# Two layers of state-space scan, router and experts on one core: the setup stage dissolved into the first scan stage

## The chip, the cores and the metric

The kernel runs on one core of a Trainium2 chip. The metric is the device time of one execution in microseconds (us). Engines are named as the profile names them: PE (matrix products), PEld (its weight loads), DVE (vector), ACT (activations), POOL (GpSimd), SP (issues the DMAs; SPq is its queue).

## What is computed

Two transformer-like layers over 4 batches of 1024 tokens with 128 channels. Each layer has an attention-like mixer and a routed feed-forward, each behind a norm that is modulated by the batch's condition vector `c`. Only the start of layer 0 matters here:

```python
# modulation, per layer l:  m = silu(c_l) @ wmod_l      (4 batches x 6 blocks of 128)
# blocks: 0 shift, 1 scale, 2 gate of the mixer;  3 shift, 4 scale, 5 gate of the feed-forward
h  = layernorm(x) * (1 + scale) + shift
xz = h @ Wi.T;  xp, z = split(xz)
xp = silu(causal_conv(xp, conv_w, 4 taps) + conv_b)
x_dbl = xp @ Wx.T;  dlt, B, C = split(x_dbl)            # rank 64, 16 states, 16 states
delta = softplus(dlt @ Wdt.T + bdt);  A = -exp(A_log)
state[n] = exp(delta * A[:, n]) * state[n] + delta * B[n] * xp          # over time, 16 states n
y = sum_n C[n] * state[n] + xp * Dp
out = (y * silu(z)) @ Wo.T;   x = x + gate * out
```

A gate has its sign kept and its size held at 0.25 or more.

## The kernel before

The whole work of layer 0's mixer is in `mamba`. Before it stands `setup` (lines 51 to 242), a block of its own that ends with all engines meeting. `setup` loads every weight and the whole of `x` (one DMA of 2 MB ahead of all others), makes the norm of all four batches (`norm.moments`, `root` with Sqrt, `normalize`, `turn`, `write`; the result is `hT`, channels on partitions), makes the modulation twice (as columns, L159, for `shift` and `scale`; as rows spread over 128 partitions by products with a broadcast stationary operand, L165, for `gate`, `shift_row`, `scale_row`), folds the convolution's taps into the weights (`wc0`, `wc1`, L209 and L210), the skip weight into the identity (`diagD0`) and prepares layer 1's parameters.

`mamba` then works batch by batch. Channels (2 halves of 128) are on partitions and time runs along the free axis in two column halves of 512 (`NCOL`). A batch has 32 **units** (`UNITS`): 16 states for each column half. One unit g is: POOL `make_bu` (L701, `u` times the spread row B), ACT `state_decay` (L605, two exps of 512 into one of 5 PSUM buffers `decay`), DVE `scan` (L786, two of 512), then the product with row C by DVE (`times_c`, L794, two) or, in each fourth unit, by POOL (L711), and PE `add_state` (L484, product with the identity into `y_ps`), which PE makes two units later. SP loads the rows B and C of each unit from DRAM into 4 and 5 buffers (L405, L414). `h` has 6 buffers: DVE's product of unit g waits for PE's `add_state` of unit g - 6.

All engines run their instructions in the order written. Beside the units of batch b stand, at fixed unit numbers s, the pieces of batch b and b + 1, all through one PSUM bank `piece`, so that each waits until ACT has read the one before: z (s = 4 to 7), x of the next batch (8 to 11, 4 taps each), ACT's Silu block with two table loads (13), low (15, 16), v (17 to 20), Exp and Ln of softplus (22 to 24), DVE's `make_delta` (24, 25), POOL's `make_u` (26, 27), the gate (17), the output product (22). Batch 0 has no batch before it: its x, low, v pieces, softplus of both column halves, `make_delta` and `make_u` (L693) are made ahead of unit 0 (lines 532 to 537, 628 to 639).

`route` (from L857) follows; its SP part loads the experts (L1056) and stores the last batch's rows (L1058), and it ends with a wait for the loads (L1064).

Of the kernel before, what the change touches and what calls it, by code (L numbers as in the profile page):

```python
# [5 lines left out]
ALU = mybir.AluOpType  # L6
# [33 lines left out]
LATE = (16, 48)  # L40
# [10 lines left out]
def setup(nc, a, m):  # L51

    with ExitStack() as ctx:
        sb = lambda name, shape, dt=F32: ctx.enter_context(nc.sbuf_tensor("su_" + name, shape, dt))
        sem = lambda name: m.kept.enter_context(nc.semaphore("su_" + name))
        ps = ctx.enter_context(nc.psum_tensor("ps_setup", [P, 8, COL], F32))
        cw0 = sb("cw0", [P, TAPS, D_IN])
        cw1 = sb("cw1", [P, TAPS, D_IN])
        wmod = sb("wmod", [P, 2, 6 * P])
        win0 = sb("win0", [P, D_IN])  # L60
        wout_raw = sb("wout_raw", [P, HALVES, P])
        cT = sb("cT", [P, 2, NBATCH])
        scT = sb("scT", [P, 2, NBATCH])
        sig = sb("sig", [P, 2, NBATCH])
        alog0 = sb("alog0", [P, HALVES, N0])
        alog1 = sb("alog1", [P, HEADS])
        dp0 = sb("dp0", [P, HALVES])
        rms = sb("rms", [P, HALVES])
        gsign = sb("gsign", [P, 2, 2, NBATCH, P])
        gate_raw = sb("gate_raw", [P, 2, 2, NBATCH, P])  # L70
        small, big, s_act, s_modT, s_modB, s_v = (
            sem(n) for n in ("small", "big", "s_act", "s_modT", "s_modB", "s_v"))
        s_bank_read = sem("s_bank_read")
        s_x = sem("s_x")
        GATE_BANK = ((0, 2), (4, 6))
        ROW_BANK = ((3, 5), (7, 1), (0, 2))
        lng = sb("lng", [P, P])
        lnb = sb("lnb", [P, P])
        s_early = sem("s_early")

        norm = make_norm(nc, ctx, m, 0, 0, [ps[:, 3, :], ps[:, 5, :]])
        block = ctx.enter_context(nc.Block())
        n_small, n_big, n_early = [0], [0], [0]

        @block.sync
        def _(sp):
            def load(dst, src, s=small, n=n_small):
                sp.dma_start(dst, src).then_inc(s, 16)
                n[0] += 1
            sp.dma_start(m.X[:], a["L0_attn_x"].rearrange("b (j p) d -> p (b j) d", p=P)).then_inc(s_x, 16)  # L90
            for l, name in ((0, "L0"), (1, "L1")):
                load(cT[:, l, :], a[name + "_cT"], s_early, n_early)
                load(wmod[:, l, :], a[name + "_wmod"], s_early, n_early)
            load(m.ident[:], a["ident"], s_early, n_early)
            load(m.tri[:], a["tri"])
            load(m.beforeb[:], a["beforeb"])
            load(m.onesb[:], a["onesb"])
            load(m.counth[:], a["counth"].partition_broadcast(P))
            load(m.count[:], a["count"].partition_broadcast(P))
            load(m.ids[:], a["ids"])  # L100
            load(cw0[:], a["L0_conv_row"].partition_broadcast(P))
            load(cw1[:], a["L1_conv_row"][:, 0:D_IN].partition_broadcast(P))
            load(win0[:], a["L0_WiT"][:, 0:D_IN])
            load(m.wz0[:], a["L0_WiT"][:, D_IN:2 * D_IN])
            load(m.tap1[:], a["tap1"])
            load(m.win1[:], a["L1_attn_W_in"][:, D_IN:D_IN + COL])
            load(m.wz1[:], a["L1_attn_W_in"][:, 0:D_IN])
            load(m.wdt1[:], a["L1_attn_W_in"][:, D_IN + COL:D_IN + COL + HEADS])
            load(m.wx[:], a["L0_WxT"].rearrange("(j p) n -> p j n", p=P))
            load(m.wdt0[:], a["L0_WdtT"])  # L110
# [2010 lines left out]
```

## Time and profile before

| | us |
|---|---|
| median of 3 runs | 1272.58 (1270.6 to 1275.98) |
| the profiled execution's own time | 1274.55 |
| its span in the profile | 1272.7 |
| `setup`, from the start to its end | 0 to 49 |
| batch 0 ahead of its units | 49 to 85.04 |
| layer 0's 128 units | 85.04 to 561 |
| route, experts, layer 1 | 561 to 1272.7 |

The chain of the page is read back from the last instruction and shows only the last 2% of the span, so the head of the kernel is read from the timeline, the windows and the waits instead.

### The profile page before, as it was taken

The page shows a single profiled execution, that of the slowest core. Times are in us where ns is not written, and L with a number is a line of the kernel's source. Part 1 is how long each engine was busy: PE and PEld are TensorE (multiplying, and loading weights), DVE is VectorE, ACT ScalarE, POOL GpSimd, SP SyncE. Part 2 cuts the span into 40 slices and gives each one's busy share as a digit, 9 for nine tenths or more (in the row PEclk, how much of TensorE's full clock was granted, in tenths as well). Part 3 has the DMA queues.
Part 4 walks back from the last instruction along what each step waited for, and adds up shares of the span by engine and source line. Part 5 has one row for each costly group of instructions (what it writes and reads, how often), then busy time and mean ns, then how long its engine had stood idle before and what let it go on. Part 6 is the DMA issues. An engine that isn't in the chain of part 4 may idle for free. (4 is left out here: it accounts for less than half of the span.)

```text
span 1272.7 us, 14828 instructions
## 1 busy us (share of the span) xinstructions
PE 897.0 (70%) x4200; PEld 569.9 (45%) x4200; DVE 919.8 (72%) x1848; ACT 590.5 (46%) x1298; POOL 767.3 (60%) x509
## 2 busy tenths in 40 slices
PE   3757877987898686762599915777786978338940
PEld 3413333433443232341599912345464756228940
DVE  6448799979988999969476744586795978464522
ACT  2264654576557646420144411546647585215620
POOL 0059679968997999830566558365534545236636
PEclk9878987997999898975699966889987968658975
DMA  6035344534643455421133411121101111142223
GB/s 173 1 104 173 120 133 149 165 115 130 179 154 125 139 164 171 138 97 44 32 86 87 81 50 44 48 57 34 44 10 42 43 50 34 34 167 59 66 58 99
DMA packets 85664, 117.72 MB, mean 92 GB/s; under 512 B 12688, under 2 KB 42576, under 8 KB 85456
## 3 DMA queue, kind: packets, MB, share of 16 engines
q1 hardware_dynamic: 78928, 103.13, 26.5%
q0 software_dynamic: 6656, 13.64, 4.9%
q8 instruction: 35, 0.57, 0.2%
q14 instruction: 45, 0.37, 0.1%
HBM read 102.52 MB, written 14.22 MB: 92 GB/s over the span
## 5 line engine op out<-in xcount | busy, mean ns | idle before, releaser
L484 PE MATMUL y_ps<-ma_h,ident 128*128 128x512 f32 x512 | 272.6, 668 | 75.4 <-POOL ma_h L711 43.6
L701 POOL TENSOR_TENSOR ma_bu<-ma_u,ma_row_b 128x1024 f32<-128x1024 f32 x128 | 298.6, 2357 | 16.8 <-DVE decay_ps L786 16.6
L605 ACT ACTIVATE decay_ps<-ma_delta,negA 128x512 f32<-128x512 f32 x256 | 173.0, 688 | 100.2 <-DVE ma_h L794 96.7
L1102 POOL DMA_INDIRECT s_rows<-xs,take x112 | 126.2, 1126 | 135.9 <-POOLq L867 78.1
L484 PEld LDWEIGHTS y_ps<-ma_h,ident 128*128 128x128 f32 x512 | 102.5, 212 | 228.1 <-issue 104.3
L786 DVE TENSOR_TENSOR_SCAN decay_ps<-decay_ps,ma_bu 128x512 f32<-128x512 f32 x96 | 115.7, 1220 | 32.1 <-ACT decay_ps L605 27.4
L1119 PE MATMUL s_up_ps<-s_xt,s_w 128*128 128x128 f32 x896 | 125.4, 286 | 7.8 <-issue 6.5
L794 DVE TENSOR_TENSOR ma_h<-decay_ps,ma_row_c 128x512 f32<-128x512 f32 x192 | 129.7, 676 | 0.0
L786 DVE TENSOR_TENSOR_SCAN decay_ps<-decay_ps,ma_carry,ma_bu 128x512 f32<-128x512 f32 x96 | 121.2, 1279 | 0.0
L1119 PEld LDWEIGHTS s_up_ps<-s_xt,s_w 128*128 128x128 f32 x896 | 115.8, 202 | 8.6 <-issue 6.8
L1128 PE MATMUL s_out_ps<-s_w,s_ht 128*128 128x128 f32 x608 | 89.6, 283 | 7.2 <-DVE s_outs L1195 7.0
L711 POOL TENSOR_TENSOR ma_h<-ma_h,ma_row_c 128x1024 f32<-128x1024 f32 x32 | 75.2, 2350 | 26.2 <-DVE ma_h L786 24.9
L1408 POOL DMA_INDIRECT mi_y<-ys,where x64 | 66.9, 1045 | 36.3 <-POOLq L1078 18.6
L1128 PEld LDWEIGHTS s_out_ps<-s_w,s_ht 128*128 128x128 f32 x608 | 78.9, 197 | 9.1 <-DVE s_ht L1185 7.3
L1146 ACT ACTIVATE s_xt<-s_xt_ps 128x128 f32<-128x128 f32 x112 | 31.8, 284 | 107.8 <-PE s_xt_ps L1111 99.1
L1438 POOL TENSOR_TENSOR mi_mm<-mi_dec,mi_gm 128x512 f32<-128x512 f32 x32 | 43.9, 1373 | 60.4 <-DVE mi_gm L1817 33.7
L1431 POOL TENSOR_TENSOR mi_cts<-mi_cdec,mi_xbc 128x512 f32<-128x512 f32 x28 | 39.2, 1400 | 65.7 <-ACT mi_cdec L1661 65.6
L1178 DVE COPY s_w<-w 128x768 f32 (+1 forms) x112 | 70.9, 638 | 5.5 <-issue 1.7
L693 POOL TENSOR_TENSOR ma_u<-ma_delta,ma_xp 128x1024 f32<-128x1024 f32 x8 | 19.7, 2458 | 86.4 <-DVE ma_delta L805 86.4
L1480 PE MATMUL mi_pre<-hT,wc 128*128 128x512 f32 x128 | 62.3, 635 | 3.9 <-ACT mi_raw L1615 1.8
L1185 DVE TENSOR_TENSOR s_ht<-s_up_ps,s_act_g 128x256 f32<-128x256 f32 x72 | 30.5, 424 | 45.1 <-ACT s_act_g L1153 24.2
L1158 ACT ACTIVATE s_ht<-s_up_ps,s_w 128x128 f32<-128x128 f32 x160 | 45.8, 370 | 27.6 <-PE s_up_ps L1119 22.4
(300 smaller groups left out, 1780.1 us busy)
## 6 DMA issues: line engine op xcount, KB each, us to landing
ma_row_b<-bc_rows SPq DMA_DIRECT2D x128, 256.0 KB, 3.6
ma_row_c<-bc_rows SPq DMA_DIRECT2D x128, 256.0 KB, 3.3
mi_cs<-cs_rows SPq DMA_DIRECT2D x32, 256.0 KB, 3.4
ys<-s_outs SPq DMA_DIRECT2D x28, 256.0 KB
w<-in_experts SPq DMA_DIRECT2D x1, 4112.0 KB, 13.4
w<-in_experts SPq DMA_DIRECT2D x1, 3072.0 KB, 10.7
xs<-rows SPq DMA_DIRECT2D x4, 512.0 KB, 3.7
out<-X SPq DMA_DIRECT2D x8, 256.0 KB
```

Of the source, the lines that this page charges most:

```text
L484: mm = pe.matmul(y_ps[:, j, :], m.ident[:], h[g % HS][:, j, :], start=False, stop=True, skip_group_check=True)
L605: act.activation(decay[s % DS][:], delta[b % 2][:, j, col(c)], ACT.Exp, scale=m.negA0[:, j, n:n + 1]).then_inc(decay_done, 1)
L701: pool.tensor_tensor(bu[g % BUS][:], u[b % 2][:, :, col(c)], both(row_b[g % BS]), ALU.mult).then_inc(bu_done, 1)
L711: pool.tensor_tensor(hs[:], hs[:], both(row_c[g % CS]), ALU.mult).then_inc(pool_product_done, 1)
L786: dve.tensor_tensor_scan(dst, d[:], bu[g % BUS][:, j, :], past, ALU.mult, ALU.add).then_inc(scan_done, 1)
L794: dve.tensor_tensor(h[g % HS][:, j, :], decay[s % DS][:], row_c[g % CS][:], ALU.mult).then_inc(product_done, 1)
L1102: pool.indirect_dma_start(rows[s % ROWS][:], None, m.xs[layer], bass.IndirectOffsetOnAxis(ap=m.take[:, s:s + 1], axis=0)).then_inc(fetched ...
L1119: mm = pe.matmul(up_ps[s % 2][:, f * P:(f + 1) * P], w[s % WS][:, f * P:(f + 1) * P], xt[s % 2][:], start=True, stop=True)
L1128: mm = pe.matmul(out_ps[s % 2][:, 0:P], ht[s % HS][:, f * P:(f + 1) * P], w[s % WS][:, UP + f * P:UP + (f + 1) * P], start=(f == 0), stop= ...
L1178: dve.tensor_copy(w[s % WS][:], m.w[layer][:, bass.ds(expert, 1), :].rearrange("p o f -> p (o f)")).then_inc(copied, 1)
L1408: pool.indirect_dma_start(fetched_rows[G % FETCH][k][:, t, :], None, m.ys[0], bass.IndirectOffsetOnAxis(ap=m.where[:, k, T:T + 1], axis=0) ...
L1480: mm = pe.matmul(bank[:], weights, m.hT[:, n, c * COL + k:c * COL + k + COL], start=(k == taps[0]), stop=(k == taps[-1]))
```

## The change

`setup` and the class `Norm` are removed; `mamba(nc, a, m)` does their work.

- The order of SP's loads is new: `cT`, the two halves of batch 0's `x`, `wmod` of layer 0 and `ident`; then eight loads that batch 0's pieces need (`taps_loaded`); then `x` of batches 1 to 3; then thirteen others (`rest_loaded`). Thirteen more are issued in batch 1's units (`later_loaded`). `cw0`, `cw1`, `wmod`, `win0`, `wout_raw` lie in `delta[1]` and `u[1]`, the normed `x` of batches 0 and 1 in `h[0]` and `h[5]`.
- Ahead of unit 0: the moments, root (Ln and Exp) and norm of batch 0; the four x pieces; low and v of the first column half alone; softplus, delta and `u` (now by DVE) of that half; moments and root of batches 1 to 3. Between the decays of unit 0 and unit 1, ACT reads batch 1's two turned pieces and two pieces of modulation rows.
- Beside batch 0's units: low, v, softplus, delta and `u` of the second column half (s = 1 to 8); the norm of batches 2 and 3 on ACT (s = 9 to 12 and 17 to 20, two tiles a unit) with their turns on PE (13, 14 and 24, 25); the gates' sign and size on 4 partitions (`modulate_rows`, s = 3 to 8, DVE); POOL's layer 1 preparation (s = 4 to 10); `wo` times the gate (`weigh_out`, s = 18 to 21, DVE).
- The modulation rows are made once, on 4 partitions, stored to DRAM (`mod_rows`, at SP's g = 11) and loaded back spread over 128 partitions: three loads of 256 KB at g = 13, eight in `route` between the experts' load and the store of the last rows.

```diff
-def setup(nc, a, m):
...
+    FIRST_LOW, FIRST_V, FIRST_SOFT, FIRST_SUM, FIRST_U = 1, 2, 5, 7, 8
+    FIRST_HAT = {2: 9, 3: 17}
+    FIRST_TURN = {2: 13, 3: 24}
+    ROWS, STORE_ROWS, LOAD_ROWS, WEIGH_OUT, FIRST_MOD, LAYER1 = 3, 11, 13, 18, 12, 4
...
+    early_keys = [("turn", 0, 0), ("x", 0, 0), ("x", 0, 1), ("turn", 0, 1), ("x", 0, 2), ("low", 0, 0), ("x", 0, 3),
+                  ("v", 0, 0), ("v", 0, 1), ("turn", 1, 0), ("turn", 1, 1), ("mod", 0, 0), ("mod", 0, 1)]
...
+                if g == STORE_ROWS:
+                    store_modulation()
+                if g == LOAD_ROWS:
+                    load_modulation()
...
+            act.wait_ge(mod_loaded, 48)
+            act.activation(scT[:], cT[:], ACT.Silu).then_inc(act_prep, 1)
             act.preload_act_table_set("natural_log_exp_and_others")
+            first_root(0, slice(0, BT))
+            act.wait_ge(prep, SCALED)
+            for key in early_keys[:7]:
+                read_piece(key)
+            act.preload_act_table_set("natural_log_exp_and_others")
+            act.activation(m.negA0[:], m.negA0[:], ACT.Exp).then_inc(act_prep, 1)
+            first_root(1, slice(BT, TILES))
+            for key in early_keys[7:9]:
+                read_piece(key)
+            soften(0, 0)
+            soften_log(0, 0)
             for j in range(HALVES):
                 state_decay(0, j)
+            for key in early_keys[9:]:
+                read_piece(key)
...
-            make_u(0, 0)
             for g in range(LEAD):
                 make_bu(g)
-            make_u(0, 1)
...
+            dve.wait_ge(first_x, 32)
+            first_moments(slice(0, BT))
+            dve.wait_ge(mod_done, 1)
...
+            for t in range(BT // 2):
+                normalize(0, t)
+            dve.wait_ge(taps_loaded, 16 * 8)
+            for k in range(TAPS):
+                then_prep(dve.tensor_tensor(m.wc0[:, k, :], win0, cw0[:, k, :], ALU.mult))
+            for t in range(BT // 2, BT):
+                normalize(0, t)
...
+            make_delta(0, 0)
+            dve.wait_ge(delta_done, 1)
+            dve.tensor_tensor(u[0][:, :, col(0)], delta[0][:, :, col(0)], xp(0, 0)[:], ALU.mult).then_inc(u_done, 1)
+            dve.wait_ge(act_prep, OTHER_ROOT)
+            for t in range(BT):
+                normalize(1, t)
...
+                for dst, block in ((m.gate[:, 0, 1], 5), (m.gate[:, 1, 1], 11), (m.lng_gate[:], 12), (m.lnb_gate[:], 13),
+                                   (m.shift_row[:, 1], 6), (m.scale_row[:, 1], 7), (m.shift_row[:, 2], 9),
+                                   (m.scale_row[:, 2], 10)):
+                    sp.dma_start(dst, m.mod_rows[:, block, :].partition_broadcast(P)).then_inc(m.late, 16)
```

## Rows read from the trace of the kernel before

**Rows 1.** Windows: busy time per engine (instructions), granted clock, DMA share, GB/s.

```profile
0.00:49.00 49.00, 23.16 (x136) 21.44 (x136) 34.16 (x139) 13.08 (x22) 0.19 (x4) 0.92 0.42 113
49.00:82.67 33.67, 25.59 (x52) 10.33 (x52) 3.79 (x6) 18.16 (x25) 3.25 (x2) 0.85 0.23 51
...
103.70:137.00 33.30, 33.26 (x72) 14.57 (x73) 24.50 (x28) 14.27 (x31) 30.41 (x15) 0.92 0.55 166
...
148.50:208.00 59.50, 47.15 (x97) 18.06 (x98) 57.85 (x66) 30.95 (x48) 49.24 (x22) 0.83 0.42 135
```

**Rows 2.** Timeline, setup: start, duration, engine, instruction, count, idle before.

```profile
11.10 6.28 DVE L192 BATCH_NORM_STATS2 stats<-X 128x6 f32<-128x128 f32 x32 [11.10 <-DMA X<-in_L_attn_x]
...
13.76 5.28 PE L159 MATMUL ps_setup<-su_scT,su_wmod 128*128 128x4 f32 x24 [13.76 <-ACT su_scT L137]
...
21.32 2.14 DVE L281 TENSOR_SCALAR n_xn<-X,n_mean,n_rstd 128x128 f32<-128x128 f32 x8
...
31.90 1.47 ACT L299 ACTIVATE hT<-ps_setup,shift,scale 128x512 f32<-128x512 f32 x2
...
32.84 5.58 PE L290 MATMUL ps_setup<-ident,n_xn 128*128 128x128 f32 x24 [6.92 <-ACT hT L299]
```

**Rows 3.** Windows of L165's matmuls alone (columns as in the first group, PE's engines).

```profile
18.90:22.00 3.10, 3.10 (x14) 3.10 (x15) 1.00 0.95 223
22.00:24.80 2.80, 2.80 (x20) 2.80 (x18) 1.00 0.11 6
```

**Rows 4.** Timeline, batch 0 ahead of its units: the pieces and the softplus.

```profile
49.23 9.73 PE L441 MATMUL y_ps<-hT,wc 128*128 128x512 f32 x16 [4.26 <-PEq L53]
...
58.80 7.03 PE L441 MATMUL decay_ps<-hT,wc 128*128 128x512 f32 x16
...
66.58 1.28 ACT L630 ACT_TABLE_LOAD   x1
...
70.94 0.68 ACT L588 ACTIVATE ma_u<-y_ps,bdt 128x512 f32<-128x512 f32 x1
...
74.93 2.05 ACT L568 ACTIVATE ma_u<-ma_u 128x1024 f32<-128x1024 f32 x2
```

**Rows 5.** Timeline, from delta to the first scan.

```profile
79.10 1.22 DVE L805 TENSOR_TENSOR ma_delta<-ma_delta,ma_u 128x1024 f32<-128x1024 f32 x1
...
82.67 6.94 POOL L701 TENSOR_TENSOR ma_bu<-ma_u,ma_row_b 128x1024 f32<-128x1024 f32 x3
85.04 2.35 DVE L786 TENSOR_TENSOR_SCAN decay_ps<-decay_ps,ma_bu 128x512 f32<-128x512 f32 x2 [4.72 <-POOL ma_bu L701]
...
89.56 2.35 POOL L693 TENSOR_TENSOR ma_u<-ma_delta,ma_xp 128x1024 f32<-128x1024 f32 x1
```

**Rows 6.** Waits from 103.7 to 158: who waited for whom, total, times, longest.

```profile
DVE decay_ps L786 <- ACT decay_ps L605: 13.2, 5, 4.4
ACT ma_xp L657 <- PE piece_ps L441: 12.0, 4, 3.3
```

**Rows 7.** Timeline of batch 0's units: PE after POOL's product, unit 12, Silu block, gate.

```profile
103.74 3.78 PE L484 MATMUL y_ps<-ma_h,ident 128*128 128x512 f32 x4 [8.59 <-POOL ma_h L711]
...
128.04 1.22 DVE L786 TENSOR_TENSOR_SCAN decay_ps<-decay_ps,ma_bu 128x512 f32<-128x512 f32 x1
...
134.84 7.03 PE L484 MATMUL y_ps<-ma_h,ident 128*128 128x512 f32 x16
...
138.16 1.28 ACT L677 ACT_TABLE_LOAD   x1
...
157.35 1.23 DVE L800 TENSOR_TENSOR ma_sz<-y_ps,ma_sz 128x1024 f32<-128x1024 f32 x1 [1.65 <-PE y_ps L484]
```

**Rows 8.** Timeline: a DVE sum with two SBUF inputs while POOL works.

```profile
186.63 2.15 DVE L805 TENSOR_TENSOR ma_delta<-ma_delta,ma_u 128x1024 f32<-128x1024 f32 x1
```

**Rows 9.** DMA issues (KB each, us to landing) and timeline rows of route.

```profile
ma_row_b<-bc_rows SPq DMA_DIRECT2D x128, 256.0 KB, 3.6
...
608.89 0.23 DVE L1051 TENSOR_SCALAR take<-r_take_ps 128x72 uint32<-128x72 f32 x1
```

More of the change, by code:

```diff
@@ new lines, in mamba @@
+    early_keys = [("turn", 0, 0), ("x", 0, 0), ("x", 0, 1), ("turn", 0, 1), ("x", 0, 2), ("low", 0, 0), ("x", 0, 3),
+                  ("v", 0, 0), ("v", 0, 1), ("turn", 1, 0), ("turn", 1, 1), ("mod", 0, 0), ("mod", 0, 1)]
+    place, placed = {}, {}
+    for key in early_keys:
+        place[key] = len(place)
+    for b in range(NBATCH):
+        for s in range(UNITS):
+            placed[b, s] = len(place)
+            for key in pieces(b, s):
+                place[key] = len(place)
+    read = lambda *key: place[key] + 1
@@ new lines, in load_x, with load @@
+            def load_x(b, part, s):
+                tiles = slice(part.start, part.stop)
+                sp.dma_start(m.X[:, b * BT + part.start:b * BT + part.stop, :],
+                             a["L0_attn_x"][b].rearrange("(t p) d -> p t d", p=P)[:, tiles, :]).then_inc(s, 16)
+            def load(dst, src, s):
+                sp.dma_start(dst, src).then_inc(s, 16)
+            load(cT[:], a["cT"], mod_loaded)
+            load_x(0, range(0, BT // 2), first_x)
+            load_x(0, range(BT // 2, BT), first_x)
@@ L520, in logits @@
                 mm.then_inc(logits_done, 1)
-            for i in range(4):
-                project_x(0, i, early[i])
-            for c in range(NCOL):
-                project_low(0, c, decay[2 + c])
-            for i in range(4):
-                project_v(0, i, early[i])
+            pe.wait_ge(act_prep, SILU_C)
+            pe.wait_ge(mod_loaded, 48)
+            columns(y_ps[:, 1, :], 0).then_inc(mod_done, 1)
+            for key in early_keys:
+                bank, before = first_banks[key]
+                if before is not None:
+                    pe.wait_ge(piece_read, read(*before))
+                if key == ("x", 0, 0):
+                    pe.wait_ge(prep, CLEARED)
+                    pe.wait_ge(prep, TAPPED)
+                if key == ("x", 0, 3):
+                    pe.wait_ge(prep, SCALED)
+                if key == ("low", 0, 0):
+                    pe.wait_ge(taps_loaded, 16 * 8)
+                if key == ("mod", 0, 0):
+                    pe.wait_ge(rest_loaded, 16 * 13)
+                make(key, bank)
             for b in range(NBATCH):
-                more = b + 1 < NBATCH
                 for s in range(UNITS):
@@ L627, in _ @@
-            for i, (j, c) in enumerate(halves):
-                act.wait_ge(piece_done, i + 1)
-                act.activation(xp(0, c)[:, j, :], early[i], ACT.Silu, bias=m.cb0[:, j:j + 1]).then_inc(piece_read, 1)
-            act.preload_act_table_set("natural_log_exp_and_others")
-            for c in range(NCOL):
-                read_low_piece(0, c, decay[2 + c], read_low(0, c))
-            for i in range(4):
-                read_v_piece(0, i, early[i], read_v(0, i))
-            soften(0)
@@ L636, in _, with make_first_hat @@
-            for c in range(NCOL):
-                soften_log(0, c)
+            def make_first_hat(b, t):
+                if t == 0:
+                    act.wait_ge(prep, SHIFTED)
+                    if b == 3:
+                        act.wait_ge(piece_done, read("turn", 2, 1))
+                tile = b * BT + t
+                act.activation(hat[:, t, :], m.X[:, tile, :], ACT.Identity, bias=shift0[:, tile:tile + 1],
+                               scale=rstd0[:, tile:tile + 1]).then_inc(hat_done, 1)
@@ L738, in modulate @@
                 if i == 0:
[L739 removed]
+                    pool.wait_ge(piece_done, read("hat", b, 1))
                 else:
```

708 lines of the change are left out of this document (364 added, 344 removed).

## The prediction

> **What bounds the kernel now.** The page's chain stops after 2% of the span, so I read the head of the kernel from the windows, then from the timeline. Up to 82.67 us POOL is busy for 3.4 us and DVE only prepares [rows 1]. The first scan starts at 85.04, released by POOL's first `make_bu`, which starts at 82.67 [rows 5]. I call that start B. All that is before B is a chain: loads, norm, pieces, softplus, delta, `u`. Behind B the units run, and there DVE is busy for 57.85 us of the 59.50 from 148.5 to 208 [rows 1], so one microsecond more of DVE there is one more in the end. In the first half of batch 0 it is different: DVE has slack, and between 103.7 and 137 PE is busy for 33.26 of 33.30 us [rows 1]. DVE waits 13.2 us in 5 places for decays, ACT 12.0 for the x pieces of PE [rows 6]. That slack matters below: work added there is partly free. So the sum has two parts: how much earlier B comes, and how much longer it is from B to the end of batch 0. What follows is left as it is.
>
> **B after the change.** *Loads.* The 2 MB of `x` land at 11.10 [rows 2]; from an issue near 0.8 that is 2.10 MB in 10.3 us, 204 GB/s with the latency in it. Up to `ident` there are now 0.97 MB: 4.8 us; I take 7.0 for their landing, since five issues and a completion lie in it. Up to the end of the eight tap loads it is 1.83 MB: 9.0 us, so 9.8. *Norm.* Silu 0.2, then four column products of two instructions each at 5.28/24 = 0.22 us [rows 2] give 1.8: 9.0, DVE's copies 9.3. In the meantime DVE has done eight statistics (6.28/32 each, 1.6 us) and its six small moments. ACT's table load (1.28) and two roots end by 9.0, too. Four tiles at 2.14/8 = 0.27 [rows 2]: 10.4. The taps (four products of 256 columns, about 0.34 each) end at 12.0 and are not late.
>
> *Clock.* The records show a granted clock of 1.00 before the first matmuls. But the same 128-column instruction takes 3.10/14 = 0.22 us until 22.0 and 2.80/20 = 0.14 after it [rows 3], so PE really starts at about half speed. I take the speed of the row at 49.23, where PE comes from a pause: 16 instructions in 9.73 against 7.03 for the next 16 [rows 4], 2.7 us lost once. The Trainium skill, "TensorE: Matmul & The Clock Gate", Part 1, says that the low level is the default and that activity releases it; the instruction times agree, the clock column of this stretch does not. By the clock column alone B would be about 3.6 us earlier.
>
> *Pieces.* The first turn (eight instructions at 5.58/24 = 0.23 [rows 2]) ends at 12.3, `hT` (0.74) at 13.1. x pieces are 8 instructions, 3.5 us at full speed [rows 4]: x0 to 19.3 with the 2.7 on top, x1 to 22.7, turn 23.7, `hT` 24.5, x2 28.0, low 29.7, x3 33.1. Now ACT carries the chain: Silu 0.7, table load 1.28 [rows 4], Exp of A 0.2, the second roots 0.5: 35.8. Two v pieces are two reads of 0.6 each: 2.4, so 38.2. Exp of 1024 columns is 1.0 [rows 4] and I take Ln alike: 40.2. Delta 1.2 and `u` on DVE the same [rows 5]: **B = 42.65**, first scan at 45.0. Against 82.67 that is 40.0 us earlier. What went: two thirds of the norm, the gates and rows at 128 partitions, the meeting of the engines at 49, half of low, v and softplus.
>
> The unseen here is the landing of many loads at once. If they run as fast as in the windows' best stretch nothing changes, since PE's chain is later anyway; if the taps come at 13 instead of 9.8, B moves by 1.5 us. If PE is at full speed from the start, B is 3.6 earlier. So B lies between 39 and 46.
>
> **From B to the end of batch 0.** Times here count from B, before and after.
>
> *Unit 1.* ACT reads batch 1's two turned pieces and two row pieces between the decays of units 0 and 1. DVE norms batch 1 after `u` (8 tiles, 2.2), PE turns them from a pause (1.9 each), then makes three small products of 512 columns at 1.7. ACT is done near 9.1, so unit 1 starts at 9.8; before, it started with DVE's next free slot, 2.4 us for the scan's start and 2.35 + 0.5 for unit 0 [rows 5], 5.2. Cost 4.6 us here.
>
> *DVE's additions, units 3 to 8.* Five operations of 512 columns at about 0.6, two small ones 0.6, `make_delta` 1.2. Sum 4.8. Where POOL works beside it, a sum with two SBUF inputs took 2.15 instead of 1.22 [rows 8]: up to 1 us more. (The Trainium skill, "SBUF — State Buffer", Who interferes with whom, says that a DVE instruction with two SBUF inputs contends with a GpSimd instruction that reads SBUF; this row is in line with it. It speaks against having the layer 1 preparation on POOL in the same units; by it the sum would be 1 to 2 us later there.)
>
> *What covers them.* Before, PE starts its closed stretch at 103.74 when POOL's first product is ready [rows 7], 21.0 after B: seven `make_bu`, the second `make_u` and the product. Without that `make_u` (2.35 [rows 5]) it is 18.6. PE's work up to the last x piece is the same, so it ends near 49.8 instead of 52.2. DVE is 6.7 us behind its old unit 8, but it no longer waits for decays: I get unit 12 at 50.2 against 45.4 (128.04 [rows 7]). ACT's Silu block needs the decay of unit 14 and so unit 12's product: 54.9 against 55.5 before (138.16 [rows 7]). So all of this, 9.4 us of it, is gone at the Silu block.
>
> *Behind the Silu block.* Here something new comes. PE's second turn of batch 2 (s = 14) waits until ACT has read the first, and ACT does so only after its Silu block, at about 63. PE stands for 6 us where it used to make four `add_state` without a pause (134.84 [rows 7]), and comes back at the low clock. Queued behind that turn are `add_state` of units 12 to 15, low and v. With 4 x 1.7 + 2 x 1.7 + 0.9, the turn itself 1.9 and 1.7 for the clock, the sum of unit 15 is ready at 77.7; before, the gate started at 74.7 and had waited 1.65 [rows 7]. **3.0 us late**. DVE then runs through. `weigh_out` (1.43 in all) moved into DVE's closed stretch: **1.4 us**. ACT's eight tiles in units 17 to 20 (3.5 us) lie in 9 us of waits for DVE: nothing, at worst 3.5.
>
> *SP.* The store of the rows waits for DVE's unit 8, then row loads of units 11 and 13 follow. They land 3.6 us after their issue [rows 9], near 45, POOL wants the one then and DVE the other at 48. The three loads of 256 KB add about 1 us each to those of unit 13, wanted at 55. Nothing, at worst 3. In `route` 2 MB more stand before the store of the last rows: at the 204 GB/s from above it lands about 10 us later, and all is wanted only when `route` ends, at 608.89 [rows 9], over 40 us after its SP part begins. Nothing.
>
> **Sum.** 40.0 - 3.0 - 1.4 = 35.6 us. Against the profiled execution's own 1274.55: 1239. The median of the runs is 2 us below that execution, well within the range, and I leave the number at 1239.
>
> **Rivals.**
> 1. *All that is moved is covered.* PE's pause behind the Silu block is caught up before the gate, or PE starts at full speed and gives back the 4 us. Time 1274.55 - 40 = 1234.5, with the clock as low as 1231. For it: 1.65 us of PE wait only. Against: PE is closed before it. Chance 0.2.
> 2. *PE, not DVE, holds batch 0 up to the gate and beyond.* Pause, low clock, and the turned pieces add up, ACT's tiles come on top (3.5), row loads slip (3), contention 1 to 2. Then 8 to 10 us more: 1248. For it: PE is busy 33.26 of 33.30 and has six turns more. Chance 0.2.
> 3. *The early start is not had.* The loads come at half the rate; the rest (5 MB) at 50 us instead of 25. Rows, low and the norm wait on them: B at 52, time 1249. Against: nothing but these loads is on the queues. Chance 0.04.
> 4. *Slower than before.* PE, more often waiting, stays at the low clock for batch 0. From the rows: 33.26 x 0.92 x 2 + 47.15 x 0.83 x 2 are 139 us against 93 of those two stretches [rows 1], 46 more, some 6 in the short stretch between and 13 ahead of B: 1304. It decides from about 35 us, that is from 70 us of PE's busy time more at the low clock than before. Against: both times when PE came from a pause, it was at full speed within some 5 us of closed work. Chance 0.02.
>
> **How the numbers follow.** Forecast 0.54 (1235 to 1244), rivals as given. The range 1229 to 1250 takes in rivals 1 and 3 and nearly all of rival 2, and the bounds of B. 0.5%, 6.4 us, is about what a measurement of this kernel can tell from no change. Faster 0.97, same 0.01, slower 0.02.
>
> **What would show it.** First scan near 45; the first x piece with instructions of 0.86 us; unit 1's decays released by ACT about 4 us after unit 0's; in the waits no DVE wait on decays between units 8 and 13; PE idle some 6 us behind the Silu block, released by ACT's read of a turned piece, and a gate that waits longer than 1.65. Batches 1 to 3 and layer 1 of the old length. Wrong would be: a first scan after 50, a wait for a load inside the chain, or batch 0's units over 10 us longer.

## The result, and the profile after

| | before | after |
|---|---|---|
| median, same chip (5 runs each) | 1275.98 (1270.60 to 1278.79) | 1258.76 (1252.35 to 1259.47) |
| ratio after / before | | 0.9861 (95% interval 0.9838 to 0.9885) |
| the profiled execution's own time | 1274.55 | 1252.35 |
| B, POOL's first `make_bu` | 82.67 | 42.71 |

The change makes the kernel 17 us faster. 35.6 had been forecast, and 1258.76 lies outside the range of 1229 to 1250. Two of the signs that the forecast had named for being wrong are there: the first scan comes after 50 (at 54.85), and batch 0's units are over 10 us longer (22.6). The profiled execution of after is the fastest of its five, so its 1252.35 flatters it: behind `route` it takes 1250.5 - 590.61 = 659.9 us where the one of before takes 1272.7 - 608.89 = 663.8 [rows 9], with nothing changed there. So what follows compares the starts of units, which are not touched by that.

The page of after, its first lines: span, then busy time of each engine.

```profile
span 1250.5 us, 14667 instructions
...
PE 878.7 (70%) x4120; PEld 552.5 (44%) x4120; DVE 925.7 (74%) x1788; ACT 594.2 (48%) x1315; POOL 771.1 (62%) x518
```

I use as markers the units whose product POOL makes (2, 6, 10, ...), since DVE scans them into `h` and the row names them; "from B" is the time since POOL's first `make_bu`.

| unit | before, from B | after, from B | longer by | forecast, from B |
|---|---|---|---|---|
| 2 | 8.7 | 21.4 | 12.7 | 4.6 |
| 6 | 21.3 | 38.0 | 16.7 | |
| 10 | 36.7 | 54.9 | 18.2 | at most 9.4 |
| 14 | 55.7 | 67.8 | 12.1 | about 0, at the Silu block |
| 18 (behind the gate) | 75.8 | 91.8 | 15.9 | 3.0 |
| 30 | 119.4 | 142.0 | 22.6 | 4.4 |

B is 40.0 us earlier, as worked out; 22.6 of these are gone by unit 30, not 4.4. So unit 30 starts 17.4 us earlier (184.71 instead of 202.10), the last marker of layer 0, unit 126, 16.7 earlier (534.63 instead of 551.32), and the median follows with 17.2. The whole miss lies between B and unit 30: 18.2 us.

Ahead of B the forecast held step by step. The timeline of after, from the loads to `u` (start, duration, engine, line, operation, count, idle before):

```profile
5.26 1.65 DVE L817 BATCH_NORM_STATS2 stats<-X 128x6 f32<-128x128 f32 x8 [4.24 <-DMA X<-in_L_attn_x]
...
7.46 0.21 ACT L587 ACTIVATE ma_scT<-ma_cT 128x8 f32<-128x8 f32 x1 [5.45 <-DMA ident<-in_ident]
...
13.09 9.47 PE L336 MATMUL decay_ps<-hT,wc 128*128 128x512 f32 x16 [1.02 <-ACT hT L496]
...
24.10 3.67 PE L336 MATMUL y_ps<-hT,wc 128*128 128x512 f32 x8 [1.10 <-ACT hT L496]
...
40.08 1.22 DVE L791 TENSOR_TENSOR ma_delta<-ma_delta,ma_u 128x1024 f32<-128x1024 f32 x1 [18.61 <-ACT ma_u L488]
```

Batch 0's `x` is there at 5.26, the last of the first five loads at 7.46 (I had 7.0). The first 16 instructions of the x pieces take 9.47 us, the next 8 take 3.67: by these durations PE starts slow here, too, and loses 2.1 us by it where I had taken 2.7 from [rows 4]. The granted clock reads 1.00 over both rows, as it did in [rows 3]. (The Trainium skill, "TensorE: Matmul & The Clock Gate", Part 1, has the low level as the default; the durations of these two rows agree with it.)

Then the place where it went wrong. Timeline of after, from B to unit 1:

```profile
42.48 12.37 DVE L832 TENSOR_SCALAR ma_h<-X,weight 128x128 f32<-128x128 f32 x8
42.71 11.54 POOL L666 TENSOR_TENSOR ma_bu<-ma_u,ma_row_b 128x1024 f32<-128x1024 f32 x5 [7.13 <-DVE ma_u L884]
54.85 2.33 DVE L770 TENSOR_TENSOR_SCAN decay_ps<-decay_ps,ma_bu 128x512 f32<-128x512 f32 x2
...
60.62 1.23 DVE L770 TENSOR_TENSOR_SCAN decay_ps<-decay_ps,ma_bu 128x512 f32<-128x512 f32 x1 [2.85 <-ACT decay_ps L552]
```

The eight norm tiles of batch 1, which stand ahead of the first scan on DVE, take 12.37 us. The same eight had taken 2.14 in `setup` [rows 2], where POOL was idle. Here POOL runs five `make_bu` in 11.54. The view of the line's instructions (ns: least, median, most; it holds batch 0's eight as well, made with POOL idle) shows that a tile is either short or as long as a whole `make_bu`:

```profile
L832 DVE TENSOR_SCALAR ma_h<-X,weight x16: 333/340/2402, 9.8 to 54.5; 128x128 f32<-128x128 f32 x16
```

Five tiles of some 2.3 and three of 0.3 make 12.4 (estimate). POOL's own instruction is not slower here (11.54/5 = 2.31 against 6.94/3 = 2.31 [rows 5]). So `first scan near 45` became 54.85, although POOL's first `make_bu` had ended near 45.0.

The same thing recurs on every small DVE instruction that the change put beside POOL. Timeline of after, the gates' rows and `weigh_out`, with the `make_bu` that runs beside the one:

```profile
74.02 2.35 POOL L666 TENSOR_TENSOR ma_bu<-ma_u,ma_row_b 128x1024 f32<-128x1024 f32 x1
74.09 2.56 DVE L843 TENSOR_SCALAR lnb_gate<-gate 4x512 f32<-4x512 f32 x1
...
80.02 0.77 DVE L845 SCALAR_TENSOR_TENSOR lnb_gate<-gate,lnb_gate 4x512 f32<-4x512 f32 x1
80.21 2.79 POOL L666 TENSOR_TENSOR ma_bu<-ma_u,ma_row_b 128x1024 f32<-128x1024 f32 x1
...
83.57 0.39 DVE L847 TENSOR_SCALAR gate<-gate 4x512 f32<-4x512 f32 x1
...
137.43 0.40 DVE L858 TENSOR_TENSOR ma_wo<-wo,gate 128x256 f32<-128x256 f32 x1
137.66 2.38 POOL L676 TENSOR_TENSOR ma_h<-ma_h,ma_row_c 128x1024 f32<-128x1024 f32 x1 [7.17 <-DVE ma_h L770]
...
140.71 1.92 DVE L858 TENSOR_TENSOR ma_wo<-wo,gate 128x256 f32<-128x256 f32 x1
...
146.11 2.29 DVE L858 TENSOR_TENSOR ma_wo<-wo,gate 128x256 f32<-128x256 f32 x1
...
151.89 2.29 DVE L858 TENSOR_TENSOR ma_wo<-wo,gate 128x256 f32<-128x256 f32 x1
```

L843 and L847 have the same form: 2.56 where it starts just behind a `make_bu`, 0.39 with POOL idle. Which of the two starts first matters: L845 starts 0.2 us ahead of a `make_bu`, keeps a short time (0.77, against 0.67 of L849, which has the same form), and it is the `make_bu` that is longer, 2.79 and not 2.35. The first `weigh_out` (0.40) starts ahead of POOL's product too, the other three behind a POOL instruction. `weigh_out` sums to 0.40 + 1.92 + 2.29 + 2.29 = 6.9 us where I had 1.4. The scans and products between them stay near 1.2 and 0.67.

The windows of after answer [rows 1] (busy time and count of PE, PEld, DVE, ACT, POOL, granted clock, DMA share, GB/s):

```profile
42.71:80.00 37.29, 22.96 (x49) 8.20 (x50) 34.44 (x32) 17.63 (x36) 28.45 (x16) 0.74 0.38 111
80.00:114.00 34.00, 31.30 (x80) 13.69 (x80) 33.12 (x38) 22.79 (x47) 29.06 (x20) 1.00 0.56 158
```

Before, PE was the closed engine of the first half of batch 0 (33.26 of 33.30) and DVE had 8.8 us of slack there. Now DVE has 0.9 us in 34 and PE 2.7. The stall and the gate look as forecast:

```profile
117.93 1.23 DVE L770 TENSOR_TENSOR_SCAN decay_ps<-decay_ps,ma_bu 128x512 f32<-128x512 f32 x1 [4.53 <-ACT decay_ps L552]
118.58 1.11 PE L362 MATMUL piece_ps<-ident,ma_hat 128*128 128x128 f32 x4 [5.71 <-ACT hT L496]
...
133.32 1.23 DVE L786 TENSOR_TENSOR ma_sz<-y_ps,ma_sz 128x1024 f32<-128x1024 f32 x1 [4.78 <-PE y_ps L412]
```

PE stands 5.71 us ahead of the second turn of batch 2 (I had 6) until ACT, done with its Silu block, has read the first; the gate waits 4.78 instead of 1.65 [rows 7], 3.1 more (I had 3.0).

### The profile page after: what moved, and what is told of

The parts are those of the page before. It is cut to its first block and busy times, and to the rows that moved or that the text cites. A ratio compares the mean times of both kernels' runs of the same rounds, so it can differ in the third digit from the quotient of the medians.

```text
span 1250.5 us, 14667 instructions
## 1 busy us (share of the span) xinstructions
PE 878.7 (70%) x4120; PEld 552.5 (44%) x4120; DVE 925.7 (74%) x1788; ACT 594.2 (48%) x1315; POOL 771.1 (62%) x518
## 5 line engine op out<-in xcount | busy, mean ns | idle before, releaser
L412 PE MATMUL y_ps<-ma_h,ident 128*128 128x512 f32 x512 | 260.0, 639 | 53.8 <-POOL ma_h L676 34.0
L412 PEld LDWEIGHTS y_ps<-ma_h,ident 128*128 128x128 f32 x512 | 97.9, 202 | 193.9 <-issue 100.3
L1202 PEld LDWEIGHTS s_out_ps<-s_w,s_ht 128*128 128x128 f32 x608 | 77.2, 193 | 10.2 <-DVE s_ht L1259 9.3
L1554 PE MATMUL mi_pre<-hT,wc 128*128 128x512 f32 x128 | 66.7, 673 | 5.1 <-ACT mi_raw L1689 2.0
L1546 PE MATMUL mi_pre<-ident,rows 128*128 128x128 f32 x64 | 14.5, 377 | 59.4 <-DVE rows L1849 55.6
## 6 DMA issues: line engine op xcount, KB each, us to landing
w<-in_experts SPq DMA_DIRECT2D x1, 3072.0 KB, 10.4
```

What stands on the lines that cost most here:

```text
L412: mm = pe.matmul(y_ps[:, j, :], m.ident[:], h[g % HS][:, j, :], start=False, stop=True, skip_group_check=True)
L1202: mm = pe.matmul(out_ps[s % 2][:, 0:P], ht[s % HS][:, f * P:(f + 1) * P], w[s % WS][:, UP + f * P:UP + (f + 1) * P], start=(f == 0), stop= ...
L1554: mm = pe.matmul(bank[:], weights, m.hT[:, n, c * COL + k:c * COL + k + COL], start=(k == taps[0]), stop=(k == taps[-1]))
```

## Experiments

The theory: a DVE instruction of the kinds `tensor_scalar` (SBUF to SBUF) and `tensor_tensor` with two SBUF inputs that starts while a POOL instruction runs stands until that one ends. That costs 10.2 us at the norm tiles, about 5 at the gates' rows (7.7 against some 2.9 by their short forms) and 5.5 at `weigh_out`; what lies ahead of the Silu block is partly taken back there, what lies behind is not. The rivals: the tiles are slow for another reason (their source still loading, their target), or a DVE that is free sooner only waits for PE and ACT, as forecast rival 2 has it. The first four kernels ran on one chip, on which before takes 1243.81 (7 runs); a control further down says what that means. The kernel after was not run on it, so what a single edit gains is read from the markers, and the whole times are given beside them.

### The tiles without POOL beside them, by order on DVE

```diff
-            make_delta(0, 0)
-            dve.wait_ge(delta_done, 1)
-            dve.tensor_tensor(u[0][:, :, col(0)], delta[0][:, :, col(0)], xp(0, 0)[:], ALU.mult).then_inc(u_done, 1)
             dve.wait_ge(act_prep, OTHER_ROOT)
             for t in range(BT):
                 normalize(1, t)
+            make_delta(0, 0)
+            dve.wait_ge(delta_done, 1)
+            dve.tensor_tensor(u[0][:, :, col(0)], delta[0][:, :, col(0)], xp(0, 0)[:], ALU.mult).then_inc(u_done, 1)
```

> The changed kernel with one move: DVE norms batch 1's eight tiles ahead of make_delta, where it was idle for 18.61 us, and not beside POOL's first make_bu. Theory (DVE and POOL share an access to SBUF, and a DVE instruction waits until POOL's running one has ended): the eight tiles take 2.2 us and not 12.37, the first scan starts near 45.1 and not at 54.85, unit 1 near 48 and not at 60.62; DVE is closed from unit 2 to 12, so most of the 10 to 12 us stays to the end of batch 0: 8 to 12 us less in the whole. Rival (the late part of batch 0 is held by PE and the gate anyway): the first scan is at 45 too, but DVE waits for decays in units 7 to 13 again and under 4 us are left. Second rival (the tiles are slow for a reason of their own): they take some 12 us here, too, and the first scan is at 55.

Measured: 1218.83 against 1243.81, ratio 0.9807 (0.9787 to 0.9827). Timeline, tiles and first scan:

```profile
34.54 2.14 DVE L832 TENSOR_SCALAR ma_h<-X,weight 128x128 f32<-128x128 f32 x8 [13.20 <-ACT weight L584]
...
44.04 2.34 DVE L770 TENSOR_TENSOR_SCAN decay_ps<-decay_ps,ma_bu 128x512 f32<-128x512 f32 x2 [2.44 <-POOL ma_bu L666]
```

The tiles are at 2.14 again, in a gap in which DVE had waited for ACT anyway, and the first scan starts at B + 2.4. Unit 14 starts at 99.49 and not 110.49, unit 30 at 173.48 and not 184.71, the last marker at 523.58 and not 534.63: 11.1 us, of which 1.05 is an earlier B (41.66). Counted from B, 12.7 us are gained at unit 2 (where the run is as far as before was), 10.0 at unit 14 and 10.2 at unit 30. So 2.7 us of this loss had been covered by the end of the Silu block's stage and 10 were left. Not all of it is contention: with the tiles earlier, unit 1 starts at B + 5.2 as before, so the 4.6 us that the forecast had charged there for the turned pieces are not paid either.

### The same tiles in their old place, with POOL held back

```diff
+            pool.wait_ge(xn_done, 2 * BT)
             for g in range(LEAD):
                 make_bu(g)
```

> The changed kernel with POOL's first make_bu held until batch 1's sixteen norm tiles of both batches are counted, DVE's order untouched. Theory (POOL's make_bu holds the tiles up): the tiles end 2.2 us after u, near 44.7, although they stand where they stood; make_bu starts there, the first scan near 47.1, unit 1 about 3 us after the reads of the turned pieces. Holding POOL back makes the kernel 5 to 10 us faster. Rival (the tiles are slow by themselves, by their addresses, by loads landing at that time or by PE reading them): they still take 12 us, and the first scan comes at about 57.

Measured: 1223.11 in one run. Timeline:

```profile
41.31 2.13 DVE L833 TENSOR_SCALAR ma_h<-X,weight 128x128 f32<-128x128 f32 x8
...
43.52 16.21 POOL L666 TENSOR_TENSOR ma_bu<-ma_u,ma_row_b 128x1024 f32<-128x1024 f32 x7 [9.11 <-DVE ma_h L833]
45.91 2.35 DVE L771 TENSOR_TENSOR_SCAN decay_ps<-decay_ps,ma_bu 128x512 f32<-128x512 f32 x2 [2.39 <-POOL ma_bu L666]
```

This tells the theory from the rivals: same place, same source and target, same time within the kernel, and 2.13 instead of 12.37. Only POOL is missing. Making POOL wait 2 us brings the last marker 8.9 us forward (525.71). In this run `u` was made 1.2 us earlier (40.17 against 41.33), so about 7.8 are due to the wait: the 10 of the run above, less the 2 of waiting.

### `weigh_out` as one instruction

```diff
-                dve.tensor_tensor(wo[:, b], m.wo0[:], m.gate[:, 0, 0, b, :].unsqueeze(1).broadcast_to([P, HALVES, P]),
-                                  ALU.mult).then_inc(wo_done, 1)
+                four = [P, NBATCH, HALVES, P]
+                dve.tensor_tensor(wo[:], m.wo0[:].unsqueeze(1).broadcast_to(four),
+                                  m.gate[:, 0, 0].unsqueeze(2).broadcast_to(four), ALU.mult).then_inc(wo_done, 1)
```

> The changed kernel with weigh_out as one instruction of 1024 columns in unit 18 in place of four of 256 in units 18 to 21 (0.40, 1.92, 2.29 and 2.29 us). Theory (each such instruction waits for POOL's running one, whatever its own size): it takes 1.2 to 3.5 us, so 3.4 to 5.7 us less at the end of batch 0 and in the whole. Rival (cost goes by size or DVE is not closed there): the same sum or no change in the whole, under 1.5 us.

Measured: 1221.14, ratio 0.9817 (0.9801 to 0.9833).

```profile
137.52 1.20 DVE L859 TENSOR_TENSOR ma_wo<-wo,gate 128x1024 f32<-128x1024 f32 x1
137.75 3.19 POOL L676 TENSOR_TENSOR ma_h<-ma_h,ma_row_c 128x1024 f32<-128x1024 f32 x1 [7.17 <-DVE ma_h L770]
```

One instruction over all four batches takes 1.20 us where the four took 6.9. Unit 18 is where it was (134.56 against 134.47), unit 30 starts at 179.31, 5.4 us earlier: behind the gate DVE is closed, and each microsecond counts. The one instruction starts ahead of POOL's product, as the first of the four had done, and POOL pays: its product takes 3.19 and not 2.38. So the run shows that one instruction in this place is cheaper than four, three of which stood behind POOL. It does not show that size is free: a sum of the same 128x1024 that starts behind a `make_bu` took 2.15 in [rows 8] and 3.31 in a run further down, against 1.22 alone.

### The turns of batch 2 ahead of the Silu block

Batch 2's norm tiles and turns come a unit earlier, and layer 1's column products (`FIRST_MOD`) move from unit 12 to unit 0 to make room.

```diff
-    FIRST_HAT = {2: 9, 3: 17}
-    FIRST_TURN = {2: 13, 3: 24}
-    ROWS, STORE_ROWS, LOAD_ROWS, WEIGH_OUT, FIRST_MOD, LAYER1 = 3, 11, 13, 18, 12, 4
+    FIRST_HAT = {2: 8, 3: 17}
+    FIRST_TURN = {2: 12, 3: 24}
+    ROWS, STORE_ROWS, LOAD_ROWS, WEIGH_OUT, FIRST_MOD, LAYER1 = 3, 11, 13, 18, 0, 4
```

> The changed kernel with batch 2's norm tiles in units 8 to 11, its turns in 12 and 13 (not 13 and 14), and layer 1's column products in unit 0. Theory (the second turn waits for ACT's read behind the Silu block and holds back four add_state): PE no longer stands there, the gate waits 1 to 2 us and not 4.78, 3 us less in the whole. Rival (the gate is late because PE comes back at the low clock or has too much work): the gate still waits over 4 us, no change in the whole.

Measured: 1226.76, ratio 0.9868 (0.9846 to 0.9890), the value of after itself. DVE's gate and PE's pause:

```profile
116.55 3.73 PE L377 MATMUL piece_ps<-ma_xp,wx 128*96 128x512 f32 x4 [4.22 <-ACT hT L496]
```

```profile
129.25 1.23 DVE L786 TENSOR_TENSOR ma_sz<-y_ps,ma_sz 128x1024 f32<-128x1024 f32 x1 [2.94 <-PE y_ps L412]
```

The wait falls from 4.78 to 2.94 and unit 30 starts at 180.65, 4.1 us earlier, but 1.1 of that is B (41.62). Of the 3.0 that are left, 1.1 is there at unit 14 already, ahead of the gate, and 1.8 is the shorter wait. PE still pauses 4.22 us, now behind both turns, and comes back at the low clock: four `low` products in 3.73, at a granted clock of 0.50. So about 3 us in the stage, and nothing that the whole time resolves. That the turn behind the Silu block holds the gate is shown for these 1.8 us; the whole of its price is not had back by this.

### All three together, with the kernel after as a control

The control is the kernel after once more, on another chip. It also answers whether markers can be compared between chips.

> The changed kernel itself, unaltered, beside the others on one chip. Expected: 0.986 of the kernel before, as measured; the eight tiles again about 12.4 us.

Measured: 1254.50 against 1274.63 (9 runs), ratio 0.9849 (0.9821 to 0.9877). Unit 30 starts at 184.56 and the last marker at 534.51, 0.15 and 0.12 us from those of the first profile. So the chip that ran the four kernels above is faster in the part behind layer 0 (there 1215.7 - 523.58 = 692 us in the first of them, here 1253.0 - 534.51 = 718), and the markers of layer 0 can be compared between chips; what varies there is B, by up to 2 us. The median saves 20.1 us here and 17.2 in the first measurement, with the same markers: a whole time tells a saving to some 3 us only.

Then all three edits in one kernel:

> The three edits together: norm tiles ahead of make_delta, weigh_out as one instruction, batch 2's tiles and turns a unit earlier. Theory (three separate losses behind DVE and PE): the gains add up at the end of batch 0, 11.2 + 5.4 + 2.6 = 19.2 us against the changed kernel, the whole near 0.971 of the kernel before. Rival (an earlier DVE only runs into the PE-bound stretch of units 7 to 13): DVE waits for decays there and 12 to 14 us are left, near 0.976.

Measured: 1239.23 (1236.00 to 1240.36), ratio 0.9713 (0.9690 to 0.9736). Timeline of DVE's two longest waits up to the gate, and of PE behind its pause:

```profile
108.52 1.23 DVE L770 TENSOR_TENSOR_SCAN decay_ps<-decay_ps,ma_bu 128x512 f32<-128x512 f32 x1 [5.06 <-ACT decay_ps L552]
...
122.03 1.22 DVE L786 TENSOR_TENSOR ma_sz<-y_ps,ma_sz 128x1024 f32<-128x1024 f32 x1 [3.10 <-PE y_ps L412]
```

```profile
109.17 3.73 PE L377 MATMUL piece_ps<-ma_xp,wx 128*96 128x512 f32 x4 [4.23 <-ACT hT L496]
...
115.43 1.88 PE L377 MATMUL piece_ps<-ma_xp,wx 128*96 128x512 f32 x4
```

Unit 30 starts at 167.92, 16.6 us earlier than in the control and 34.2 earlier than before. Counted from B, which is late in this run (43.43), it is 17.4 earlier than in the control; the single gains, counted so, add to 10.2 + 5.5 + 3.0 = 18.7. The gains nearly add up, and the markers exclude the rival's 12 to 14 us, although DVE does wait for decays again in units 12 and 13 (0.70 and 1.06). The kernel is faster than before and than after. That its 35.4 us are so near the forecast's 35.6 is in part luck. The tiles and `weigh_out` without their contention account for 15.7 of the 18.2 us missed; the earlier turns give 3.0 back that the forecast had counted as spent, while the rows' contention (8.2 us of rows where I had 3.6) is still in it. From B, unit 30 is 5.1 us later than before, where I had 4.4. The two PE rows are the same four products at a granted clock of 0.50 and of 1.00, 1.85 us apart; I had put 1.7 for that.

The same kernel ran twice more, as the partner of later experiments:

> The kernel with the three edits again, as the mark for the next run on the same chip: near 0.971 of the kernel before.

Measured: 1241.74 against 1274.72, ratio 0.9752 (0.9724 to 0.9781); unit 30 at 164.87.

> The kernel with the three edits, as the mark on this chip: near 0.973 of the kernel before.

Measured: 1240.14 against 1276.59, ratio 0.9711 (0.9691 to 0.9732); unit 30 at 166.67. The three medians save 35.4, 33.0 and 36.5 us. From B, unit 30 is 18.5 and 17.6 us earlier in these two than in the control.

### What are the gates' rows worth?

In the kernel with all three edits the rows still stand beside POOL. First they move to POOL itself, in eight instructions at units 3 to 6, with the layer 1 preparation behind them:

```diff
-                if b == 0 and LAYER1 <= s < LAYER1 + TAPS + HALVES + 1:
+                if b == 0 and ROWS <= s < ROWS + 4:
+                    modulate_rows(2 * (s - ROWS))
+                    modulate_rows(2 * (s - ROWS) + 1)
+                if b == 0 and LAYER1 <= s < LAYER1 + TAPS + HALVES + 1:
...
-                    if b == 0 and ROWS <= s < ROWS + 6:
-                        modulate_rows(s - ROWS)
```

> As the run with the three edits, and the gates' rows (scale plus one, sign, size, the two norm rows) are made by POOL in its units 3 to 6, in eight instructions, not by DVE (7.7 us there in the changed kernel); layer 1's preparation starts at POOL's unit 7. Theory (DVE sets the pace there, POOL has some 10 us to spare): another 3 to 7 us less. Rival (PE and ACT set the pace of units 7 to 13 once DVE is early; or POOL, late with make_bu, makes DVE wait): within 1.5 us of that run, DVE's waits for decays or for make_bu being longer by what it saves.

Measured: 1246.74, ratio 0.9780 (0.9749 to 0.9810), against 1239.23 of its partner on the same chip: 7.5 us worse, where the expectation had 3 to 7 better and its rival no change. POOL's timeline, the windows of both (first this kernel, then its partner, the same columns as above), and two waits, of ACT and of DVE:

```profile
56.24 1.49 POOL L715 TENSOR_SCALAR gate<-gate 4x512 f32<-4x512 f32 x1
57.82 1.93 POOL L717 TENSOR_SCALAR lnb_gate<-gate 4x512 f32<-4x512 f32 x1
```

```profile
42.00:92.00 50.00, 38.62 (x74) 15.52 (x75) 39.25 (x42) 27.91 (x61) 49.10 (x29) 0.80 0.44 126
92.00:117.00 25.00, 20.77 (x52) 9.15 (x52) 14.42 (x16) 19.61 (x35) 24.61 (x19) 0.93 0.54 167
```

```profile
42.00:92.00 50.00, 39.81 (x87) 16.10 (x88) 47.52 (x53) 32.30 (x69) 48.41 (x29) 0.90 0.46 132
92.00:117.00 25.00, 20.77 (x49) 8.94 (x48) 17.93 (x20) 19.21 (x33) 22.53 (x12) 0.86 0.54 182
```

```profile
87.00 0.69 ACT L501 ACTIVATE ma_xp<-piece_ps,cb 128x512 f32<-128x512 f32 x1 [8.41 <-POOL ma_u L657]
...
89.32 1.22 DVE L794 TENSOR_TENSOR_SCAN ma_h<-decay_ps,ma_bu 128x512 f32<-128x512 f32 x1 [4.80 <-issue]
```

A row costs 1.49 on POOL, against 0.39 on an undisturbed DVE, and POOL was full in this stretch already (48.41 of the 48.57 us from the partner's B, 43.43, to 92). It is now closed until 117. Its `make_u` comes 5.6 us later, counted from B, and ACT stands 8.41 us for it; behind ACT, DVE waits 12.0 us for decays between 42 and 117 (7.1 in the partner), and 4.80 more at 89.32, for which the profile names nobody. DVE's busy time falls from 47.52 to 39.25. Unit 14 starts at 106.06 and not 100.54. The contention is not gone either: DVE's `make_delta`, which meets POOL at another place, takes 3.31 and not 1.21.

Then four of the six kinds of row work, those that form the gates' sign and size, are left out of the computation, to bound what any better place could give:

```diff
-                elif i == 1:
-                    then_prep(dve.tensor_scalar(size, gates, -1.0, 0.25, ALU.mult, ALU.max))
-                elif i == 2:
-                    then_prep(dve.scalar_tensor_tensor(size, gates, 1.0, size, ALU.mult, ALU.max))
-                elif i == 3:
-                    then_prep(dve.tensor_scalar(gates, gates, 0.0, 2.0, ALU.is_ge, ALU.mult))
-                elif i == 4:
-                    then_prep(dve.scalar_tensor_tensor(gates, gates, -1.0, size, ALU.add, ALU.mult))
```

> The kernel with the three edits, and the four DVE instructions that make the gates' sign and size in units 4 to 7 left out (about 6.2 us of DVE there, 3.8 of it contention or waiting; the gates are then the raw products, so the output is another). Theory of the prediction (what DVE is spared ahead of unit 12 is lost again in waits for decays, since PE's x pieces and ACT's Silu block set that stretch): unit 10 is 5 to 6 us earlier from the first make_bu, unit 14 and the end of batch 0 by under 2.5. Rival (DVE sets the pace up to the Silu block): unit 14 and the end are 5 to 6 us earlier, too.

Measured: 1238.97, ratio 0.9726 (0.9701 to 0.9751), its partner 0.9752 (0.9724 to 0.9781) on the same chip. First the partner, then this kernel:

```profile
61.28 2.38 DVE L843 TENSOR_SCALAR lnb_gate<-gate 4x512 f32<-4x512 f32 x1
...
67.74 1.21 DVE L770 TENSOR_TENSOR_SCAN ma_h<-decay_ps,ma_bu 128x512 f32<-128x512 f32 x1
```

```profile
64.43 1.23 DVE L770 TENSOR_TENSOR_SCAN decay_ps<-decay_ps,ma_bu 128x512 f32<-128x512 f32 x1 [1.40 <-ACT decay_ps L552]
...
66.16 1.21 DVE L770 TENSOR_TENSOR_SCAN ma_h<-decay_ps,ma_bu 128x512 f32<-128x512 f32 x1
```

The four are worth 4.25 us of DVE here (the expectation took 6.2). Taken away, a wait for a decay comes up at once (1.40) and unit 6 is only 1.6 us earlier; unit 10 is 2.1 earlier, where the expectation had 5 to 6, unit 14 1.6 and unit 30 0.5, both under the 2.5 of the expectation. So most of this row work is covered once DVE is not 10 us late for another reason.

Last, the layer 1 preparation on POOL begins at unit 10 and not 4, so that POOL has gaps beside the rows:

```diff
-    ROWS, STORE_ROWS, LOAD_ROWS, WEIGH_OUT, FIRST_MOD, LAYER1 = 3, 11, 13, 18, 0, 4
+    ROWS, STORE_ROWS, LOAD_ROWS, WEIGH_OUT, FIRST_MOD, LAYER1 = 3, 11, 13, 18, 0, 10
```

> The kernel with the three edits, and POOL's layer 1 preparation from its unit 10 on and not from its unit 4. POOL is busy for 49.76 of 50 us from 42 to 92 in the kernel with the three edits, and the preparation has some 4 us of that. Theory (POOL, closed there, holds DVE up by late make_bu and by the shared access): DVE's instructions in units 3 to 9 are shorter by 1 to 2 us and unit 10 is 2 to 4 us earlier, of which under 1.5 are left at the end of batch 0, as PE and the Silu block take the rest. Rival (the preparation was free in its place): unit 10 within 1 us; or, put later, it meets the shorter slack of units 10 to 16 and costs 1 to 3 us.

Measured: 1239.58, ratio 0.9705 (0.9686 to 0.9724), its partner 0.9711 (0.9691 to 0.9732). Timeline and window:

```profile
61.45 1.69 DVE L843 TENSOR_SCALAR lnb_gate<-gate 4x512 f32<-4x512 f32 x1
...
66.58 1.64 DVE L845 SCALAR_TENSOR_TENSOR lnb_gate<-gate,lnb_gate 4x512 f32<-4x512 f32 x1
```

```profile
42.00:92.00 50.00, 45.12 (x91) 18.35 (x92) 48.00 (x49) 31.95 (x71) 43.89 (x22) 0.83 0.49 128
```

POOL has 6 us of gaps now (43.89 of 50), and L843 falls to 1.69 from its partner's 2.38; but L845 rises from 0.77 to 1.64 and the last two rows (L853) from 1.77 to 3.89, so that the rows sum to 10.4 and not 8.2. The contention has moved and grown: where `make_bu` run back to back, a row that lands behind one waits for it. From B, unit 10 is 2.4 us later, as the expectation's rival had it and against its theory, unit 14 is 0.4 later, and the whole is the same.

## Why the prediction was wrong by half

*Right.* B (42.65 forecast, 42.71 measured), with the landing of the loads not late, the slow start of PE, and each piece of the chain to within 0.7 us. That it fits to 0.06 is luck: in the runs whose kernel is the same up to there, B lies between 41.6 and 42.8. Unit 1's decays are released by ACT, PE stands some 6 us behind the Silu block (5.71), the gate waits 3.1 us longer (3.0). The loads, SP's store and what `route` had added cost nothing: `take` is reached at 590.61, 18.3 earlier than before, no less than unit 126's 16.7.

*Wrong, the step "Unit 1".* It has "DVE norms batch 1 after `u` (8 tiles, 2.2)". The 2.2 is from [rows 2], read where POOL was idle; the tiles were moved to where POOL starts its longest run of `make_bu`. They took 12.37. Unit 1 started at B + 17.9 and not 9.8. The two experiments that keep POOL away gave back 11.1 and 8.9 us at the last marker, 10.0 and 7.8 of it not by an earlier start.

*Wrong, the term of `weigh_out`.* 1.4 forecast, 6.9 measured; one instruction instead of four gave 5.4 us back. Of the miss of 18.2 us these two terms are 10.2 + 5.5 = 15.7 by their own durations; no run splits the 2.5 that are left between the rows and the Silu block.

*Wrong in size, without a price of its own shown, "DVE's additions".* The rows took 7.7 us where their short forms make some 2.9 (estimate) and the forecast had 3.6, not the "up to 1 us more" of the forecast. The 0.6 for a row was not taken from any row; it was near enough (0.39 and 0.67). I had a row for this contention, [rows 8] with 2.15 instead of 1.22, and read the 0.9 in it as a share of the instruction. It is what was left of POOL's instruction: the `make_bu` of this row of before ended at 187.69, and the sum, begun at 186.63, ended at 188.78, about its own length behind that.

```profile
185.34 2.35 POOL L701 TENSOR_TENSOR ma_bu<-ma_u,ma_row_b 128x1024 f32<-128x1024 f32 x1
```

The Trainium skill, "SBUF — State Buffer", Who interferes with whom, says that DVE instructions with two SBUF inputs contend with a GpSimd one that reads SBUF, that `tensor_scalar` in the modes with two ports does too, and that the one that issues first has the shared ports for its whole instruction while the other blocks fully and is not just slowed. The trace agrees in both directions: tiles of 0.33 took up to 2.40 behind a `make_bu`, and POOL's product took 3.19 instead of 2.38 behind `weigh_out`. I had cited it for the second input, at one place of the change, and not held it against each of the DVE instructions that were moved.

*Wrong, the step "all of this is gone at the Silu block".* At unit 10 after is 18.2 us longer from B than before, at unit 14 still 12.1: the block took 6.1. It takes back what PE and ACT need time for in any case; from 80 to 114 DVE is idle for 0.9 us, and there is no more to hide behind. In the kernel with the three edits the step holds in the main: from B, unit 10 is 6.0 us later than before and unit 14 only 1.4, and taking away 4.25 us of DVE gains 1.6 there. Even so its Silu block starts at B + 57.6, where I had 54.9.

Of the rivals, the first did not occur. The second is nearest, but has neither the size (8 to 10 us more had been its price, 18 were found) nor the mechanism: PE did not hold batch 0, DVE did. It named "contention 1 to 2" as its smallest part. The third and fourth did not occur. The slower rival's low clock is seen behind a pause, in the rows of the combined kernel at 109.17 (granted clock 0.50) and no longer at 115.43 (1.00).

*Open.* Whether what blocks a `tensor_scalar` and what blocks a two-input `tensor_tensor` is one mechanism: no run separates them. What the rows alone cost in the kernel after (the runs took them from the improved kernel only). The rest of the gate's wait: 2 to 3 us after both turns stand ahead of the Silu block.

## What to carry to other kernels

A duration read where another engine is idle is not the duration where it works: for each DVE instruction that moves, ask which POOL instruction will run beside it and which of the two will start first. If it is a `tensor_scalar` or has two SBUF inputs and starts second, price it at the rest of POOL's instruction plus its own time, however small it is; if it starts first, POOL pays. Put such work into a wait of DVE ahead of POOL's first instruction (10 us here), hold POOL for 2 us (8 us), or merge four into one that starts ahead of POOL's (5 us); moving it onto a POOL that is full costs more than it saves. And a cover that hides work is only as long as the late engine has slack in it: count it again after all added times, not before.

## What the runs showed of the hardware

- A DVE `tensor_scalar` from SBUF to SBUF, or one with two SBUF inputs, that starts while a POOL `tensor_tensor` runs ends with it plus about its own time: `tensor_scalar` 128x128 from 0.33 to as much as 2.40 us, 4x512 from 0.39 to 2.56, `tensor_tensor` 128x256 from 0.40 to 2.29, 128x1024 from 1.21 to 3.31.
- If it starts first, it keeps its time and POOL's is the longer one: `make_bu` 2.79 and not 2.35, POOL's product 3.19 and not 2.38 beside a `weigh_out` of 1.20.
- DVE's scans and products with one input in PSUM stayed at 1.2 to 1.3 and at 0.65 to 0.68 with POOL at work.
- POOL takes 1.49 us for a `tensor_scalar` of 4x512, against 0.39 on an undisturbed DVE.
- The same four products take 3.73 us at a granted clock of 0.50, after a pause of 4.23, and 1.88 some 6 us later, at 1.00.
